# Second weights loaded transposed, half of their products moved into the step of maxima, magnitudes crossed by TensorE, first batch normalised in the setup

## The reference

```python
x = x + attention(layernorm(x))      # 16 heads of 16, scores masked to a band
x = x + mixture(layernorm(x))        # 8 experts, hidden 512, best 2 of 8 per row
```

## Time and profile before

| | us |
|---|---|
| median of 3 runs | 1502.41 |
| profiled execution, its own time | 1499.72 |
| its span | 1498.0 |
| setup block | 0 to 63.72 |
| lead-in, to the first round of maxima | 63.72 to 105.47 |
| to the first exponentials | 105.47 to 140.84 |
| attention steps | 140.84 to 895 |
| tail of the attention | 895 to 941.1 |
| experts | 941.1 to 1498.0 |

### The profile page before, as it was taken

The page is one execution under the profiler, slowest core; times in us unless marked ns, Lnnn a source line. Parts: engine busy times, 40 slices in busy tenths (PEclk is TensorE's granted clock), DMA queues, the critical chain, the costliest instruction groups (busy, mean ns, idle before and its releaser), DMA issues. The chain is left out here.

```text
span 1498.0 us, 46577 instructions
## 1 busy us (share of the span) xinstructions
PE 1250.4 (83%) x18216; PEld 912.0 (61%) x18216; DVE 971.0 (65%) x2065; ACT 804.2 (54%) x1404; POOL 648.3 (43%) x682
## 2 busy tenths in 40 slices
PE   6667888887788878877778772799999999999996
PEld 5534454554444545544445331688888888888885
DVE  4224678676776787667767655466666666666664
ACT  1354765667456665665455530355555555555554
POOL 2031421536355435363443646244445445554445
PEclk9868999998898998889988665899999999999999
DMA  6455464554544536445554232456664485464443
GB/s 131 167 128 149 97 186 106 170 130 131 160 137 134 161 100 195 129 120 147 122 152 107 88 100 89 110 70 118 123 121 64 65 175 69 64 122 67 66 65 48
DMA packets 226026, 175.35 MB, mean 117 GB/s; under 512 B 129082, under 2 KB 193082, under 8 KB 225866
## 3 DMA queue, kind: packets, MB, share of 16 engines
q1 hardware_dynamic: 167050, 116.62, 31.3%
q0 software_dynamic: 25728, 33.78, 13.1%
q10 hardware_dynamic: 33088, 22.71, 5.7%
HBM read 66.32 MB, written 89.40 MB: 104 GB/s over the span
## 5 line engine op out<-in xcount | busy, mean ns | idle before, releaser
L988 DVE TENSOR_REDUCE mx<-p_max 128x4 f32<-128x736 f32 (+1 forms) x256 | 219.0, 856 | 173.9 <-PE p_max L1259 173.7
L815 ACT ACTIVATE probs<-p_exp,unscale 128x736 f32<-128x736 f32 (+1 forms) x256 | 210.1, 821 | 173.2 <-PE p_exp L1259 168.4
L1509 PE MATMUL p_h<-xt_parts,w_hi 128*128 128x256 f16 x1824 | 273.8, 273 | 2.2 <-DVE xt_parts L1597 2.1
L1601 DVE SCALAR_TENSOR_TENSOR t<-p_h,b,t 128x256 f32<-128x256 f32 x272 | 131.0, 484 | 159.9 <-ACT t L1548 155.4
L1646 POOL DMA_INDIRECT out<-yw,tokens x136 | 212.2, 1561 | 28.3 <-POOL tick L1645 18.3
L1645 POOL TENSOR_TENSOR tick<-tick 128x1 f32<-128x1 f32 x136 | 82.8, 609 | 265.6 <-ACT yw L1565 265.6
L1548 ACT ACTIVATE t<-p_h,b,undo 128x256 f32<-128x256 f32 x272 | 148.4, 558 | 90.8 <-PE p_h L1509 84.9
L1509 PEld LDWEIGHTS p_h<-xt_parts,w_hi 128*128 128x128 f16 x1824 | 178.0, 98 | 24.0 <-DVE t L1601 2.7
L1509 PE MATMUL p_h<-xt_parts,w_lo 128*128 128x256 f16 x912 | 174.0, 273 | 0.0
L1290 PE MATMUL p_out<-probs,v 64*32 64x184 f32 (+1 forms) x4096 | 147.9, 349 | 4.1 <-DVE out_t L998 4.0
L711 POOL DMA_INDIRECT routed<-rows,slots x128 | 128.9, 1007 | 47.7 <-issue 47.5
(11 more groups left out here) (244 smaller groups left out, 2628.7 us busy)
## 6 DMA issues: line engine op xcount, KB each, us to landing
qk_dram<-qk_hi SPq DMA_DIRECT2D x128, 128.0 KB, 2.4
qs<-qk_dram SPq DMA_DIRECT2D x64, 192.0 KB, 5.0
ks<-qk_dram SPq DMA_DIRECT2D x64, 192.0 KB, 4.9
x_in<-in_x SPq DMA_DIRECT2D x64, 128.0 KB, 3.5
qk_dram<-qk_lo SPq DMA_DIRECT2D x64, 128.0 KB, 2.6
w_mat<-in_W ACTq DMA_DIRECT2D x32, 256.0 KB, 4.1
out<-x_sb SPq DMA_DIRECT2D x64, 128.0 KB
w_split<-w_first_hi SPq DMA_DIRECT2D x24, 256.0 KB
```

The lines of the kernel that those rows point to most:

```text
L815: nc.scalar.activation(probs[r % 3][:, :, 0:hi - lo].rearrange("p (e s) w -> p e s w", e=2), p_exp[:, :, 0:2 * WIN].rearrange("p e (s w) - ...
L988: nc.vector.tensor_reduce(out=maxes, in_=p_max[:, :, 0:2 * WIN].rearrange("p e (s w) -> p e s w", s=2)[:, :, :, 0:hi - lo], axis=AX.X, op= ...
L1509: last = nc.tensor.matmul(p_h[:, m % KC, k, :], w[e][a][:, k, HID * c + P * m:HID * c + P * m + P], xt[:, x, c, :], start=(n == 0 and c == ...
L1601: nc.vector.scalar_tensor_tensor(t3[m // 2][:, m % 2, :], p_h[:, m % KC, 1, :], kept["b13"][:, 1, e, m:m + 1], t1[m][:], ALU.add, ALU.mult ...
```

## The change

- The host lays out W2 transposed, and b2, the biases, Wg and W_o as the kernel wants them: one load each, no transposes in TensorE, no copies `w2_t` in ScalarE.
- Of the eight products with Wf, four (`EARLY`) stay in the setup, from four buffers that lie in `qs`. The other four are done in the step of maxima in eight halves, in the rounds `LATE_ROUNDS`, from buffers that the first batches don't need yet, to `p_out`; ScalarE copies each half and stores it. The b2 rows come last in the setup.
- The magnitudes are crossed by a transpose on TensorE, a maximum, a diagonal matrix and a matmul with ones, the sum of the fluctuations by another; GpSimd's two all-reduces go. GpSimd fills one `ks` and all three `v` afterwards, VectorE the other `ks`.
- SP loads batch 0 first, and the setup normalises it to `xn`. Batch 1 is loaded at the end of the setup's queue.
- Rounds 0 to 15 of the maxima alternate between `p_max` and `p_exp`.
- Every scattered row carries all eight gates (18 words in place of 6); the wait and the copy between the two choices go; ScalarE picks its gate by the expert's number. `choose` keeps `gates` whole and uses `others` for the second choice.

```diff
-META = 6
-
-M_TOKEN, M_GATE, M_SECOND = 0, 2, 4
-USED = 4
+META = 2 + 2 * 8
+
+M_TOKEN, M_GATES = 0, 2
+USED = META
...
+MAG_COLS = 32
+EARLY = 4
+LATE_ROUNDS = (4, 5, 7, 10, 11, 13, 14, 15)
...
+def max_buffer(r, p_max, p_exp):
+
+    return p_exp if r < ROUNDS and r % 2 else p_max
...
+        w2_t = [keep["qs"][e // 2][:].rearrange("p a s -> p (a s)").bitcast(F32)[:, MAT * (e % 2):MAT * (e % 2) + MAT].rearrange(
+            "p (c h) -> p c h", c=NC) for e in range(EARLY)]
...
+            def load_x(b):
+                for t in range(NT):
+                    sp.dma_start(xt[b][:, t, :], io["x"][b, P * t:P * t + P, :]).then_inc(s_x[b], 16)
...
+            load_x(0)
...
+            sp.dma_start(wo_blocks[:], io["W_o"]).then_inc(s_rest, 16)
+            sp.dma_start(bv_cols[:], io["bv"]).then_inc(s_rest, 16)
...
-            for h in range(H):
-                p0, e, half, seg = HD * (h % PAIRS), h % 2, h // 2 % 2, h // 4 % 2
-                c0 = 32 * (2 * e + seg) + HD * half
-                sp.dma_start(wo_blocks[p0:p0 + HD, h // PAIRS, c0:c0 + HD],
-                             io["W_o"][h].rearrange("d k -> k d"), allow_slow_non_contiguous=True).then_inc(s_wo, 16)
...
+            pool.wait_ge(s_mv1, 1)
+            nc.gpsimd.tensor_tensor(keep["rs1"][:], keep["var1"][:], keep["neg_half"][:], ALU.pow)
+            pool.drain()
+            nc.gpsimd.tensor_tensor(keep["shift1"][:], keep["less1"][:], keep["rs1"][:], ALU.mult).then_inc(s_rs1, 1)
...
             nc.gpsimd.memset(keep["ks"][1][:], M_SCALE)
-            nc.gpsimd.memset(keep["v"][2][:], 1.0)
-
-            pool.wait_ge(s_mag, 1)
-            nc.gpsimd.partition_all_reduce(mag_all[:], mag[:], P, bass.bass_isa.ReduceOp.max).then_inc(s_all, 1)
-            pool.wait_ge(s_flu, 1)
-            nc.gpsimd.partition_all_reduce(fluct_all[:], fluct[:], P, bass.bass_isa.ReduceOp.add).then_inc(s_all, 1)
+            for p in range(3):
+                nc.gpsimd.memset(keep["v"][p][:], 1.0)
...
+            act.wait_ge(s_ld, 16 * LD)
+            for e in range(EARLY):
+                act.dma_start(w2_t[e], io["W2"][e].rearrange("(c p) h -> p c h", p=P)).then_inc(s_w2[e], 16)
+            act.wait_ge(s_rs1, 1)
+            for t in range(NT):
+                last = nc.scalar.activation(xn[:, t, :], xt[0][:, t, :], ACT.Identity, bias=keep["shift1"][:, t:t + 1], scale=keep["rs1"][:, t:t + 1])
+            last.then_inc(s_xn, 1)
+            sigmoid_exp(0)
+            sigmoid_exp(1)
...
+            pe.wait_ge(s_mag, 1)
+            nc.tensor.transpose(p_set[0:MAG_COLS, T_BANK, 0:P], mag[:], keep["ident"][:]).then_inc(s_magt, 1)
+            pe.wait_ge(s_diag, 1)
+            nc.tensor.matmul(p_set[:, ALL_BANK, 0:MAG_COLS], ones[0:MAG_COLS, :], mag_diag[:], start=True, stop=True)
+            pe.wait_ge(s_flu, 1)
+            nc.tensor.matmul(p_set[:, ALL_BANK, MAG_COLS:MAG_COLS + 2], ones[:], fluct[:], start=True, stop=True, skip_group_check=True).then_inc(s_all, 1)
+
+            pe.wait_ge(s_b2, 32)
+            for e in range(EARLY):
+                pe.wait_ge(s_w2[e], 16)
+                if e >= 2:
+                    pe.wait_ge(s_wfc, e - 1)
+                for k in range(KC):
+                    for c in range(NC):
+                        last = nc.tensor.matmul(p_w2f[:, e % 2, k, :], w2_t[e][:, c, P * k:P * k + P], wf[:, c, :],
+                                                start=(c == 0 and k % 2 == 0), stop=(c == NC - 1), skip_group_check=True)
+                last.then_inc(s_wf, 1)
...
+            pe.wait_ge(s_wfc, EARLY)
...
+            dve.wait_ge(s_magt, 1)
+            nc.vector.tensor_reduce(out=mag_top[:], in_=p_set[0:MAG_COLS, T_BANK, 0:P], axis=AX.X, op=ALU.max)
+            dve.drain()
+            nc.vector.tensor_scalar(mag_diag[:], keep["ident"][0:MAG_COLS, 0:MAG_COLS], mag_top[:], None, ALU.mult).then_inc(s_diag, 1)
...
+            nc.vector.tensor_scalar(mag_all[:], p_set[:, ALL_BANK, 0:N_MAG], 2.0 ** -60, None, ALU.max)
...
-                nc.gpsimd.tensor_copy(words[:, :, M_GATE:M_GATE + 2].bitcast(F32)[:, :, 0], gw[0][:])
-                nc.gpsimd.tensor_copy(words[:, :, M_SECOND:M_SECOND + 2].bitcast(F32)[:, :, 0], gw[1][:]).then_inc(s_noted, 1)
+                nc.gpsimd.tensor_copy(words[:, :, M_GATES:META].bitcast(F32), gates[:]).then_inc(s_noted, 1)
...
-                if j:
-                    words = rows[b % 3][:, :, 2 * D:ROW]
-                    pool.wait_ge(s_scat[b % 3], 128 * (b // 3) + 64)
-                    nc.gpsimd.tensor_copy(words[:, :, M_GATE:M_GATE + 2].bitcast(F32)[:, :, 0],
-                                          words[:, :, M_SECOND:M_SECOND + 2].bitcast(F32)[:, :, 0])
-                    pool.drain()
...
+            def load_late_weights():
+                for n in range(LATE):
+                    act.dma_start(w2_t[n], io["W2"][EARLY + n].rearrange("(c p) h -> p c h", p=P)).then_inc(s_w2, 16)
+
+            def keep_late(h):
+                act.wait_ge(s_wfp, h + 1)
+                wait(act, s_w2f[h % 2], 16 * (h // 2))
+                nc.scalar.activation(out_t[:, h % 2, :], p_out[:, h % 2, :], ACT.Copy).then_inc(s_wfc, 1)
+                act.wait_ge(s_wfc, h + 1)
+                act.dma_start(io["w2f"][EARLY + h // 2, :, S * (h % 2):S * (h % 2) + S], out_t[:, h % 2, :]).then_inc(s_w2f[h % 2], 16)
...
+            load_late_weights()
             for b in range(LEAD_BATCHES):
-                norm(b)
+                if b:
...
-                wait(pe, s_mx, r)
-                masked_scores(p_max, n, qs[b % 2], ks[b % 2], 3 * HD).then_inc(s_sc, 1)
+                wait(pe, s_mx, r - 1 if r <= ROUNDS else r)
+                masked_scores(max_buffer(r, p_max, p_exp), n, qs[b % 2], ks[b % 2], 3 * HD).then_inc(s_sc, 1)
...
+                    wait(pe, s_mx, ROUNDS)
...
+            def late_product(h):
+                n, half = h // 2, h % 2
+                if half == 0:
+                    pe.wait_ge(s_w2, 16 * LATE)
+                wait(pe, s_wfc, h - 1)
+                for k in (2 * half, 2 * half + 1):
+                    for c in range(NC):
+                        last = nc.tensor.matmul(p_out[:, half, D * (k % 2):D * (k % 2) + D], w2_t[n][:, c, P * k:P * k + P], wf[:, c, :],
+                                                start=(c == 0 and k % 2 == 0), stop=(c == NC - 1), skip_group_check=True)
+                last.then_inc(s_wfp, 1)
...
+                    if i == FIRST_STEP and n in LATE_ROUNDS:
+                        keep_late(LATE_ROUNDS.index(n))
                     if split_expert(i) is not None:
                         if n in (0, 2):
                             spread_magnitudes(split_expert(i), n // 2)
@@ -985,12 +992,15 @@
                     filled(dve, s_full, "M", b - 2, 0)
                 dve.wait_ge(s_sc, r + 1)
                 maxes = mx[:, b % 2, 0:Q].rearrange("p (e s k) -> p e s k", e=2, k=NK)[:, :, 2 * gk:2 * gk + 2, k]
-                nc.vector.tensor_reduce(out=maxes, in_=p_max[:, :, 0:2 * WIN].rearrange("p e (s w) -> p e s w", s=2)[:, :, :, 0:hi - lo],
+                nc.vector.tensor_reduce(out=maxes, in_=max_buffer(r, p_max, p_exp)[:, :, 0:2 * WIN].rearrange("p e (s w) -> p e s w", s=2)[:, :, :, 0:hi - lo],
                                         axis=AX.X, op=ALU.max).then_inc(s_mx, 1)
 
             def take_out(b, gk):
 
 
+                if b == 0 and gk == 0:
+                    for half in range(2):
+                        dve.wait_ge(s_w2f[half], 16 * LATE)
                 if gk == 0:
                     filled(dve, s_full, "D", b - 1, 1)
                 dve.wait_ge(s_pv, ROUNDS * b + NK * gk + NK)
@@ -1003,10 +1013,10 @@
                 blocks = out_t[:].rearrange("p h (c r) -> p h c r", r=32)
                 nc.vector.reciprocal(sums[:], blocks[:, :, :, HD])
                 dve.drain()
-                nc.vector.tensor_tensor(att_t[:].rearrange("p (c h d) -> p h c d", h=2, d=HD), blocks[:, :, :, 0:HD],
+                nc.vector.tensor_tensor(att_t.rearrange("p (c h d) -> p h c d", h=2, d=HD), blocks[:, :, :, 0:HD],
                                         sums[:, :, :, None].to_broadcast([P, 2, S // 32, HD]), ALU.mult)
                 dve.drain()
-                nc.vector.transpose(att[:, gk, :], att_t[:]).then_inc(s_att, 1)
+                nc.vector.transpose(att[:, gk, :], att_t).then_inc(s_att, 1)
 
             def residual(b, k):
                 if k == 0:
@@ -1045,25 +1055,25 @@
                 dve.drain()
                 nc.vector.reciprocal(gs[:], gs[:])
                 dve.drain()
+                wait(dve, s_noted, b)
                 nc.vector.tensor_tensor(gates[:], ge[:], over_experts(gs), ALU.mult)
 
             def choose(b, j):
 
+                left = (gates, others)[j]
+                dve.drain()
+                nc.vector.tensor_reduce(out=gw[j][:], in_=left[:], axis=AX.X, op=ALU.max)
+                dve.drain()
```

(64 more changed lines are left out.)

220 lines of the change are left out of this document (93 added, 127 removed).

## The result

The changed kernel takes **1456.32 us** (median of 4 runs, 1451.97 to 1461.26) against 1504.58 (4 runs, 1496.77 to 1507.93): ratio 0.9687, 95% interval 0.9636 to 0.9738. A second set gave 0.9698 (0.9674 to 0.9721). The profiled execution took 1451.97, span 1450.2, 47.8 less than the span before; 28.5 less was forecast. The 1456 lies under my low end of 1459.

What follows compares the result with a forecast made beforehand. Bounds taken by stage: the setup a chain through all engines, then a wait for the first batch, then TensorE and VectorE alternating. -14.2 - 11.1 + 0.6 + 1.5 - 5.3 = -28.5 from 1499.7 gave 1471.2, stated as 1473 us; range 1459 to 1486.

Steps and rivals of the forecast that it cites:

- low end: Whole kernel: 1459 us, from the memsets holding nothing, a warm lead-in and -3 us in the step of maxima.
- Steady steps: Attention steps: the scatter's second half no longer waits or copies, nobody waits for it; 0 us, bounds -3 and +3.
- Setup: Block before attention: fewer transposes and products on TensorE, end at 49.5 us against 63.7; -14.2 us.
- rival 1: Setup: GpSimd's memsets hold no VectorE operations, the chain ends at 23.6, product 2 follows warm; 1467 us, chance 0.20.
- the chain's end: Setup: VectorE's small operations, held by GpSimd's memsets until 20.3 us, finish at 28.0; without the hold 23.6.
- Product 2: Setup, TensorE: waits for ScalarE's first copy, starts at 29.3 us after over 5 us idle, takes 5.4 at half clock.
- First batch and lead-in: Setup's end to first maxima: only the block change stays before the first transposes, -11.1 us; lead-in at its old clock.
- late loads: Lead-in: ScalarE first issues four loads of the late weights, delaying its first copy; +0.6 us.
- Step of maxima: Stage before the first exponentials: the double buffer removes TensorE's waits, eight half products come in; +1.5 us, bounds -3 and +13.
- rival 2: Step of maxima: TensorE at half clock becomes the bound, or stores delay ScalarE's queue; 1481 us, chance 0.17.
- Tail: After the last attention step: the last two batches scatter without the gap between halves, twice 2.65; -5.3 us.
- Rival 4: Experts: reading 36 bytes of gates per token costs time; 0.42 us more per tile cancels the gain; chance 0.05.

Runs made afterwards that it cites:

- e9: Changed kernel without VectorE's subtraction of the largest logit before the exponential of the gates; 0.9687 of the kernel before.
- e2: Changed kernel with the old routing (1036-byte rows, two noted gates, wait and copy between scatters); 0.9804 of the kernel before, which took 1561.06 us there.
- e6: Changed kernel with the VectorE operations seen held by GpSimd (gates, lg, var, x2n, two of w_inv) written as scalar_tensor_tensor; 0.9854 of the kernel before.
- e1: Kernel before with the routing part of the change alone; 0.9979 of the kernel before, which took 1561.06 us in that set.
- e12: Changed kernel with GpSimd's four large memsets (ks, v) behind the end of VectorE's magnitude chain; 1450.62 us, 0.965 of the kernel before.
- e13: Changed kernel as it is, run again as the anchor of its set; 1457.11 us, 0.9698 of the kernel before.
- e5: Changed kernel as it is, run again at the level where every kernel took 4 to 5% more; 0.9837 of the kernel before.
- e7: Changed kernel with e6's scalar_tensor_tensor forms and GpSimd's four large memsets behind VectorE's magnitude chain; 0.9834 of the kernel before.
- e4: Kernel before with rows of 1060 instead of 1036 bytes and nothing else; 1.0011 of the kernel before, which took 1561.06 us there.

## Why the prediction was wrong

**The step that failed** is "Steady steps": "0, bounds -3 and +3 by the clock's drift". Measured: 15.1 us in the profile, 17 between the exponentials. GpSimd's idle half was true, and nobody waits for its scatter; but a change of its times moves its large operations against VectorE's small ones. I had counted that hold in the setup and left it out of sixteen steps. Step 5 before, by its timeline:

```profile
371.97 2.05 POOL L733 TENSOR_TENSOR rows<-x2n,rows 128x1024 f16<-128x1024 f32 x1
373.24 2.92 DVE L1048 TENSOR_TENSOR gates<-ge,gs 128x32 f32<-128x32 f32 x1
374.00 2.11 POOL L721 TENSOR_TENSOR w_first_lo<-w_mat,w_first_hi 128x1024 f16<-128x1024 f32 x1
...
379.01 0.42 PE L1252 MATMUL p_max<-mask,ident_bf 64*64 64x248 bf16 x4 [4.07 <-DVE mx L988]
```

and after:

```profile
345.49 2.12 POOL L709 TENSOR_TENSOR w_first_lo<-w_mat,w_first_hi 128x1024 f16<-128x1024 f32 x1
345.70 1.95 DVE L1059 TENSOR_TENSOR gates<-ge,gs 128x32 f32<-128x32 f32 x1
...
350.50 0.30 PE L1263 MATMUL p_max<-mask,ident_bf 64*64 64x248 bf16 x4 [3.10 <-DVE mx L995]
```

GpSimd is 1 us further in its order, the gates are held 1 us less, the row maxima behind them come 1 us sooner, TensorE idles 3.10 for 4.07 us and goes on at 0.30 for 0.42 a group. That is how a step can get shorter. Over all steps, between the first and the last exponential, VectorE's operations that lie more than 0.3 us above the median of their line all end with a GpSimd operation. What they take above it is 54.6 us in both profiles of before, 51.2 and 51.7 with the routing alone, 44.4 and 47.9 with the rest alone, 46.0 and 45.7 with both. The largest part is not the gates but the second norm, `x2n` (L941, now L948), 22.0 us and then 16.0, and TensorE waits for it less. The waits of that stretch before:

```profile
PE p_sh L1215 <- DVE x2n L941: 34.9, 15, 3.8
PE p_exp L1252 <- DMA qs<-m_rows: 7.8, 7, 1.9
```

and after:

```profile
PE p_sh L1226 <- DVE x2n L948: 29.1, 15, 3.8
PE p_exp L1263 <- DMA qs<-m_rows: 4.9, 7, 1.7
```

The second profiles have 36.2 and 31.2 for `x2n` (e9, though, 34.8). The wait for the row of maxima is 4.8 to 6.5 us in the kernels with the new setup and 6.9 to 8.9 in those without. TensorE's idle time in the stretch falls by 8.4 us in all and its busy time by 7.8. So the holds and the waits behind them shrink along with the steps; no experiment took the holds away, and on the slower level the two go together poorly (held time 33.9 and stretch 798.4 in e2, but 47.5 and 822.5 in e6, 53.9 and 804.8 in e1). How much of the 15 us the holds are worth, and why TensorE waits less for the row of maxima, **stays open**.

**Setup**: -14.2 forecast, -16.3 measured. The hold was forecast to 20.3 and ended at 19.7, the chain's end at 28.0 was right, so rival 1 is out. Wrong was "Product 2 waits for that copy ... more than 5 us of idle TensorE, and so at half clock": the products start 5.7 us later than I had them, too late for that gap. Late start and missing gap nearly cancelled: the last product ends at 36.4, where I had 38.2. That is luck.

**First batch and lead-in**: transposes at 47.80 for 76.05, -28.3, where -25.3 was forecast; the late loads cost 0.8 (0.6). I had named 2 us for a lead-in at full clock and not counted them; from the transposes to the first maxima 1.2 us are gained, with the 0.8 of the late loads taken off already (mean clock 0.70 for 0.63).

**Step of maxima**: +0.8 (+1.5). Right in size. The half products take 2.0 us each and not 1.8, but all at the same full pace (mean clock 1.00 in this stage), so rival 2 is out. By the first exponentials 28.6 us are gained, where 23.2 were forecast.

**Tail**: -4.9 (-5.3). The eight indirect issues follow 1.27 us apart, twice, where the earlier trace rows had the gap:

```profile
869.64 0.96 POOL L699 DMA_INDIRECT routed<-rows,slots  x1 [0.30 <-issue]
870.91 0.96 POOL L699 DMA_INDIRECT routed<-rows,slots  x1 [0.30 <-issue]
```

**Experts**: 557.67 for 556.9, and the earlier trace rows has become

```profile
ACT tokens L1600 <- DMA words<-routed: 15.7, 5, 4.0
```

Rival 4 (0.42 us a tile) is out: the experts take 0.01 a tile more. That 8 and 36 bytes are both under the Trainium skill's line-rate bound ("DMA: Bandwidth & Descriptors", the specifications table) fits that.

The account: 14.2 was 16.3; 11.1 - 0.6 with the lead-in was 13.2; +1.5 was +0.8; 0 was -15.1; -5.3 was -4.9; the experts +0.8. Some 15 of the 19 us that I missed stand in one line. Two sums of the prediction were off by 1 us or less: the low end adds up to 1460 and not 1459, and round 3 to 107.9 and not 107.7.

## What to carry to other kernels

When two engines hold one another, a saving on the idle one may not be free of effect: look at which of its long operations begin before the other's short ones, in every step, and give the term both signs and a size from the longest hold. Put fills on GpSimd behind the other engine's chain of small operations; here that alone gave 6.5 us (in the set of e12 and e13; none showed between e5 and e7). And follow each engine's written order before you say when a product starts: a small matmul ahead of it decides.

## What the runs showed that I had not expected

Back-to-back GpSimd operations hold VectorE as one: the end of one memset and three more 7.44 us, and in e6 the rest of one `w_first_lo`, `rows` and another `w_first_lo` together 5.97, with no operation let in between. The Trainium skill ("SBUF — State Buffer", "Who interferes with whom") has the holding last for one whole instruction; the trace shows it last over a row of them.

The slower level shows itself inside groups of TensorE. The sixteen weighings of one round have one record of weight loads in the first profile of the changed kernel, just before step 5:

```profile
337.73 0.18 PEld L1304 LDWEIGHTS p_out<-probs,v 64*32 64x32 f32 x16
```

and three in e5, the same kernel in the same place:

```profile
343.12 0.20 PEld L1304 LDWEIGHTS p_out<-probs,v 64*32 64x32 f32 x10 [0.17 <-issue]
343.82 0.20 PEld L1304 LDWEIGHTS p_out<-probs,v 64*32 64x32 f32 x5 [0.50 <-issue]
345.25 0.12 PEld L1304 LDWEIGHTS p_out<-probs,v 64*32 64x32 f32 x1 [1.22 <-issue]
```

TensorE stops between matmuls of one group and waits for nothing that the profile shows. Stops of over 0.4 us like these are 47 to 60 in the steps of every kernel of that level, old setup or new, 31 to 39 us in all, and none to three on the faster level; some two thirds fall in every other step. At the place shown scatters and the load of `qs` run, but they do in the first profile too. The operation `lg<-lg,gm` is held there for some 6 us in four or five steps (up to 8.9 in e4; e2 has one such step only), where the first profile shows one. That the stops make it late, and so let it meet GpSimd, is a guess. The chip that the record numbers 13 showed both levels in different sets, so a level need not belong to a chip. What the stop waits for wasn't tried.
